# Two pre-norm layers on one core: batch 2's norm and router ahead of the expert blocks, a shared half moved between the two batches

## The chip, the cores and the metric

The kernel runs on 1 core of one Trainium2 chip. The time is the device time of one execution in microseconds; 906.62 us is the median of three runs of the kernel before (905.75 to 911.3).

## What is computed

Input: 2 sequences (batches) of 1024 tokens with 128 features. Four steps follow, each with a layer norm in front and a residual add behind:

```python
x = x + _L0_attn_ref(_layernorm(x), ...)   # latent attention, 8 heads, softmax over 1024 keys
x = x + _L0_ffn_ref(_layernorm(x), ...)    # shared expert + 2 of 8 routed experts, width 352
x = x + _L1_attn_ref(_layernorm(x), ...)   # causal attention with rotary positions, 16 heads of 8
x = x + _L1_ffn_ref(_layernorm(x), ...)    # per batch 2 of 8 experts, chosen by token 0
```

The second step is `silu(x @ gate.T) * (x @ up.T) @ down.T` for the shared expert and, by a softmax router, for the top two experts of each token, weighted by their normed probabilities. The third step needs queries, keys and values of `x` after the second.

## The kernel before

The 2048 tokens are 16 tiles of 128, and four chunks of 512 (c = 0 to 3; chunks 0 and 1 are batch 1, chunks 2 and 3 batch 2). Each engine has its own instruction list, written out by hand, and the lists meet only in semaphore waits. So the place of a call in each of the five lists sets the order of the work.

**The routed experts.** A router (`gate_logits` on PE, `probabilities`, `probabilities_normed`, `ranks`, `slots`, `block_experts`, `shares` on DVE, `gate_exps` on ACT, `expert_counts` on PE) gives each token two slots in a list that is sorted by expert and padded to blocks of 128. GpSimd (POOL) scatters the normed rows to memory (`scatter`, L580, 16 indirect DMAs a batch). 23 blocks a batch (`NB`), 46 in all (`N_ALL`), then run one after the other: SyncE loads them in quads of four blocks (`load`, L453, and `store`, L462, alternate in one queue), PE turns a quad (`block_x_turns`, L1435), ACT and DVE split it in a high and a low part (`block_x_hi`, `block_x_lo`), and for each block PE makes gate and up (`block_up`, six matmuls), ACT the silu (L939), DVE the product (`block_hidden`, L2250), PE turns it (`block_h_turns`) and multiplies down (`block_down`), ACT copies the result (`block_y`). In the loop over i (L1481, L954, L2257), block i + 1's gate and up are issued ahead of block i's turns. The weights' low parts are subtracted on POOL (`low_weights`, L572, L577) before the first block. The norm of batch 2, its turns (`second_turns`, L1223), logits and router stand inside the loop, at the blocks that `XNT_AT`, `GATE_AT`, `SOFTMAX_AT`, `RANKS_AT`, `COUNTS_AT`, `SLOTS_AT`, `EXPERTS_AT` and `SHARES_AT` name (L163).

**The shared expert** goes by chunks: `shared_up(c)` (L1377, six matmuls of 512 columns), `shared_silu` (L902), `shared_hidden` (L2115), `shared_down(c)` (L1390, 24 matmuls of 128 columns), `shared_add` (L2123). Chunks 0 and 1 come before the blocks, 2 and 3 behind them (L1490 to L1665).

**The fronts.** When a batch's blocks are stored, POOL gathers each token's two rows (`gather`, L588, 8 indirect DMAs a chunk), DVE mixes them into x (`mix`), norms (`norm_op`), PE turns (`front_turn`) and makes q, k and v (`front_qkv`), and the rotation follows (`front_rope` on DVE, `second_rope` on POOL). Fronts 0 and 1 stand in the loop of blocks 31 to 45 (`FRONT_MIX` and the like, L158), fronts 2 and 3 in attention units 0 to 2 (`SECOND_FRONT`, `FRONT_QKV_UNIT`).

**Attention of the second layer** runs in 8 units of four heads, units 0 to 3 for batch 1. POOL stages keys, queries and values of a unit (`stage_keys`, `stage_queries`, `stage_values`, L633 to L646), PE turns them (`turn_stack`, L1514), ACT copies them into stacks of float32r (L982, L988; the key stacks must be cleared before: `keys_zero`, L694 and L695). A unit needs the maxima of its scores first: 40 slots (`MX1`) of `scores_max1` on PE (L1544) and `maximum1` on DVE (L2307 masked, L2310 plain). `MX1_HALF` = 28 of unit 0's come ahead of it, the rest and those of the next unit go between its own score matmuls (`scores1`, L1564) as `first_slot(u, place)` paces them: a unit has ten steps (k) of four places each. ACT takes the exponentials (L1000), POOL masks the diagonal (L655), PE multiplies with the values (`values1`, L1581).

What follows in POOL's list is strictly in order: before, it is `scatter(0)`, `low_weights`, `scatter(1)`, `gather(0)`, clears, staging of units 0 and 1, `gather(1)` (16 DMAs), `stage_keys(2)`, masks.

## Time and profile before

| what | us |
|---|---|
| median of three runs | 906.62 |
| all runs | 905.75, 911.3, 906.62 |
| the profiled execution, its own time | 908.84 |
| its span, first to last instruction | 906.8 |
| PE busy (matmuls), share of the span | 805.3, 89% |
| DVE busy | 590.1, 65% |
| ACT busy | 515.9, 57% |
| POOL busy | 385.8, 43% |
| mean granted clock of TensorE, of full | 0.946 |

The span leaves out some 2 us of the execution's time around the first and the last instruction. A busy share is a mean over stages that have different limits, and waiting of an engine costs only where it is the one that the others wait for. TensorE's granted clock is one of two levels, 2.4 GHz (1.00) and 1.2 GHz (0.50); a value between is a mean over a stretch with both. In a timeline row, the first number is the start from the span's begin, the second the time from the first to the last of its merged instructions, and the brackets give how long the engine stood before it and who released it.

### The profile page before, as it was taken

How to read it: one execution, taken by the hardware profiler on the slowest of the kernel's cores; microseconds unless marked ns; L12 is line 12 of the kernel's file. 1: busy time of each engine (PE TensorE's matmuls, PEld its weight loads, DVE VectorE, ACT ScalarE, POOL GpSimd, SP SyncE). 2: the span in 40 equal slices, each digit the busy share in tenths (PEclk: the TensorE clock that was granted, in tenths of full speed). 3: DMA queues.
4: the chain of work that ended last, by engine and by line, in shares of the span. 5: the costliest groups of instructions: out<-in, count | busy, mean ns of one | idle time of the engine just before them, and what ended most of it. 6: DMA issues, size and time to landing. Idle time of an engine off the chain costs nothing. (4 is left out here: it accounts for less than half of the span.)

```text
span 906.8 us, 13841 instructions
## 1 busy us (share of the span) xinstructions
PE 805.3 (89%) x4634; PEld 471.4 (52%) x4634; DVE 590.1 (65%) x1552; ACT 515.9 (57%) x891; POOL 385.8 (43%) x420
## 2 busy tenths in 40 slices
PE   5889899998999988868799977899999999999858
PEld 2354343443444432568798654455555555554436
DVE  5967677686776826536326567887778778776151
ACT  3335565656656665336465533467776777676641
POOL 3406675666754754821542375236444223112100
PEclk9979999999999989989899997699999999999969
DMA  9400000000000000101232002000000000000001
GB/s 355 154 1 0 1 1 1 1 1 1 1 1 1 1 1 10 61 12 56 82 97 65 35 19 76 1 1 1 2 0 2 1 1 1 1 1 1 1 0 47
DMA packets 13789, 24.86 MB, mean 27 GB/s; under 512 B 3319, under 2 KB 8313, under 8 KB 13466
## 3 DMA queue, kind: packets, MB, share of 16 engines
q1 hardware_dynamic: 11048, 18.36, 5.8%
q0 software_dynamic: 2048, 4.20, 1.5%
q10 hardware_dynamic: 626, 1.43, 0.5%
q8 instruction: 40, 0.66, 0.3%
q14 instruction: 27, 0.22, 0.1%
HBM read 14.54 MB, written 9.44 MB: 26 GB/s over the span
## 5 line engine op out<-in xcount | busy, mean ns | idle before, releaser
L1854 DVE TENSOR_REDUCE mx_part<-ps 128x1 f32<-128x512 f32 x256 | 163.2, 681 | 68.3 <-PE ps L1166 67.5
L1000 ACT ACTIVATE pt<-ps 128x1024 f32<-128x1024 f32 (+1 forms) x160 | 149.4, 939 | 75.1 <-PE ps L1564 73.9
L795 ACT ACTIVATE pt<-ps 128x512 f32<-128x512 f32 x256 | 141.1, 596 | 85.1 <-PE ps L1191 77.1
L1544 PE MATMUL ps<-rounded 128*128 128x512 f32 (+3 forms) x384 | 140.1, 403 | 15.7 <-DVE mx_part L2307 7.6
L738 ACT ACTIVATE rounded<-ps 128x512 fp32r<-128x512 f32 (+3 forms) x166 | 97.9, 591 | 86.8 <-PE ps L1520 24.6
L2307 DVE CUSTOM_DVE_ANT_0 ps<-ps,later 128x128 f32<-128x128 f32 (+3 forms) x256 | 119.9, 516 | 26.8 <-PE ps L1544 25.4
L1191 PE MATMUL ps<-rounded 100*128 100x512 f32 x256 | 123.0, 494 | 13.5 <-ACT pt L795 12.6
L1564 PE MATMUL ps<-rounded 128*128 128x512 f32 (+3 forms) x384 | 130.1, 379 | 0.0
L655 POOL TENSOR_SCALAR_AFFINE_SELECT pt<-pt 128x512 f32<-128x512 f32 x64 | 40.0, 638 | 189.4 <-ACT pt L1000 189.4
L1166 PE MATMUL ps<-rounded 98*128 98x512 f32 x256 | 104.2, 425 | 11.2 <-DVE rounded L1847 7.7
L1544 PEld LDWEIGHTS ps<-rounded 128*128 128x128 f32 x384 | 71.8, 198 | 55.2 <-DVE mx_part L2310 22.6
L2310 DVE TENSOR_REDUCE mx_part<-ps 128x1 f32<-128x512 f32 x128 | 82.3, 685 | 23.9 <-PE ps L1544 23.8
L1564 PEld LDWEIGHTS ps<-rounded 128*128 128x128 f32 x384 | 70.8, 194 | 43.5 <-issue 19.9
L1191 PEld LDWEIGHTS ps<-rounded 100*128 100x128 f32 x256 | 48.0, 192 | 84.8 <-ACT pt L795 48.5
L533 POOL TENSOR_TENSOR xn<-pt 128x512 f32<-128x512 f32 x48 | 60.5, 1283 | 59.2 <-ACT pt L795 59.2
L1581 PE MATMUL ps<-pt,v_cur 128*9 128x512 f32 (+3 forms) x768 | 78.5, 497 | 1.5 <-POOL pt L655 1.5
L1199 PE MATMUL ps<-pt,ckv 128*32 128x512 f32 x512 | 74.3, 655 | 0.9 <-ACT pt L795 0.9
L533 POOL TENSOR_TENSOR xnT<-pt 128x512 f32<-128x512 f32 x48 | 60.5, 1281 | 33.3 <-ACT pt L795 33.3
L1166 PEld LDWEIGHTS ps<-rounded 98*128 98x128 f32 x256 | 49.1, 194 | 36.3 <-issue 17.4
L584 POOL DMA_INDIRECT to_experts<-xn,slot_i x32 | 31.8, 994 | 55.5 <-DVE slot_i L2082 46.4
L2250 DVE TENSOR_TENSOR pt<-ps,pt 128x352 f32<-128x352 f32 x46 | 24.1, 523 | 46.4 <-ACT pt L939 43.8
L738 ACT ACTIVATE pt<-ps 128x128 f32<-128x128 f32 (+2 forms) x96 | 37.5, 393 | 26.4 <-PE ps L1465 14.2
(286 smaller groups left out, 1250.3 us busy)
## 6 DMA issues: line engine op xcount, KB each, us to landing
wm<-in_wm SPq DMA_DIRECT2D x1, 4896.0 KB, 15.7
to_experts<-kstage SPq DMA_DIRECT2D x6, 512.0 KB, 4.6
of_experts<-pt SPq DMA_DIRECT2D x12, 256.0 KB, 2.0
kstage<-to_experts SPq DMA_DIRECT2D x10, 256.0 KB, 3.4
wm<-in_experts SPq DMA_DIRECT2D x1, 1028.0 KB
x<-in_x SPq DMA_DIRECT2D x4, 256.0 KB, 5.8
out<-x SPq DMA_DIRECT2D x4, 256.0 KB, 2.3
early<-in_wo ACTq DMA_DIRECT2D x1, 512.0 KB
```

The lines of the kernel that those rows point to most:

```text
L533: nc.gpsimd.tensor_tensor(sums(u, j)[i], pt0(0, i), pt0(1, i), ALU.add).then_inc(pair_add, 1)
L738: return nc.scalar.activation(dst, src, ACT.Copy)
L795: nc.scalar.activation(pt0(k, i), ps[:, ST0_BANKS[i % 2], :], ACT.Exp, scale=SCALE0).then_inc(exp_done, 1)
L1000: nc.scalar.activation(pt[:, 4 * (t % 2) + 2 * g:4 * (t % 2) + 2 * g + 2, 0:w], ps[:, ST1_BANKS[2 * g]:ST1_BANKS[2 * g] + 2, 0:w], ACT.Exp ...
L1166: mm(ps[:, max_bank(u, n), :], cq[0:NZ, b * S + j * P:b * S + (j + 1) * P], key_stack[u % 2][0:NZ, h, c * CH:(c + 1) * CH], start=True, st ...
L1191: mm(ps[:, ST0_BANKS[i % 2], :], key_stack[pp][0:NZM, h, k * P:(k + 1) * P], query_stack[pp][0:NZM, h, c * CH:(c + 1) * CH], start=True, s ...
L1544: ins = mm(bank[:, o:o + w], query_stack1[pp][:, i * P:(i + 1) * P], key_stack1[pp][:, r, c * CH:c * CH + w], start=(o == 0), stop=(o == p ...
L1564: ins = mm(ps[:, ST1_BANKS[r], o:o + w], key_stack1[pp][:, r, j * P:(j + 1) * P], query_stack1[pp][:, q0:q0 + w], start=(o == 0), stop=(o ...
L1581: ins = mm(ps[RS * r:RS * r + DH + 1, CTX_BANK, CH - w:CH], v_cur[pp][:, j, r, :], pt[:, 4 * (t % 2) + r, o:o + w], start=(j == CTX1_START ...
L1854: v.tensor_reduce(mx_part[u % 2][:, o:o + 1], ps[:, max_bank(u, n), :], AX_X, ALU.max).then_inc(max_done, 1)
L2307: v.tensor_tensor_reduce(tile, tile, later[:, CH - w:CH], 1.0, NEG, ALU.add, ALU.max, dst).then_inc(max1_done, 1)
L2310: v.tensor_reduce(dst, tile, AX_X, ALU.max).then_inc(max1_done, 1)
```

## The change

- `norm_chunk(2)`, `norm_chunk(3)`, batch 2's turns, its logits and its softmax leave the loop of the blocks and stand ahead of it; `block_x_turns(0)` goes in front of the wait for the weights' low parts. Ranks, counts, slots, experts and shares of batch 2 move from blocks 6 to 12 to blocks 0 to 6.
- Chunk 2's shared half moves from behind the blocks to between block 22 and block 23 (`SHARED_AT`); there, block 22 is finished (turned, multiplied down, copied) before block 23's gate and up. Chunk 3's up part begins at block 45, its down part lies between the first stack turns.
- Fronts 0 and 1 come two blocks sooner, so that all of front 1, rotation included, lies in the loop. Front 3's mixes and norm are done two steps a place from place 33; the turns and q/k/v of fronts 2 and 3 shift by some places.
- POOL: unit 0's keys are staged ahead of the clears; one of the two key stacks is cleared by ACT; unit 1's staging comes behind `gather(2)`; `gather(3)` is split in pairs behind unit 0's first masks, with `stage_keys(2)` after the third pair.
- `first_slot` gives unit 0 five maxima a step instead of six, over more steps, and two of them come ahead of the unit.

The core of the diff:

```diff
 def first_slot(u, place):
-    return MX1_HALF + place + (2 * HG if u else min(2 * HG, (place + 1) // 2))
+    return MX1_HALF + place + (2 * HG if u else 2 + min(2 * HG - 2, place // HG))
...
-FRONT_MIX, FRONT_STATS, FRONT_RSTD, FRONT_XN = ((31, 32), (37, 38)), (33, 39), ((34, 35), (40, 41)), (36, 42)
-FRONT_TURN, FRONT_QKV, FRONT_ROPE = (36, 42), (37, 43), (43, 46)
-
-FRONT_QKV_UNIT = {(6, 1): 0, (7, 1): 1, (8, 0): 2, (9, 1): 3}
-SECOND_FRONT = {2: (4, 2), 3: (20, 1)}
-XNT_AT, GATE_AT, SOFTMAX_AT, RANKS_AT, COUNTS_AT, SLOTS_AT, EXPERTS_AT, SHARES_AT = (1, 2), 3, (4, 5), (6, 7), 8, 9, 10, (11, 12)
+FRONT_MIX, FRONT_STATS, FRONT_RSTD, FRONT_XN = ((29, 30), (35, 36)), (31, 37), ((32, 33), (38, 39)), (34, 40)
+FRONT_TURN, FRONT_QKV, FRONT_ROPE = (34, 40), (35, 41), (41, 44)
+
+SECOND_TURN = {(0, 6, 1): 2, (1, 6, 0): 3}
+SECOND_QKV = {(0, 7, 1): (2, 0), (0, 8, 0): (2, 1), (0, 9, 1): (2, 2), (1, 1, 1): (2, 3),
+              (1, 6, 1): (3, 0), (1, 7, 1): (3, 1), (1, 8, 0): (3, 2), (1, 9, 1): (3, 3)}
+SHARED_AT = {NB - 1: 2, N_ALL - 1: 3}
+SECOND_FRONT = {2: (6, 2), 3: (33, 2)}
+RANKS_AT, COUNTS_AT, SLOTS_AT, EXPERTS_AT, SHARES_AT = (0, 1), 2, 3, 4, (5, 6)
...
@@ POOL
             gather(0)
+            gather(1)
...
             pool.wait_ge(x_turn, Q_ALL)
             nc.gpsimd.memset(kstage[1][:].bitcast(F32), 0.0).then_inc(stage_fixed, 1)
+            pool.wait_ge(rope_step, 2 * (NCH // B) - 1)
+            pool.wait_ge(stage_fixed, 1)
+            stage_keys(0, 0)
             pool.wait_ge(bu_mm, N_ALL)
-            nc.gpsimd.memset(qstage[1][:].bitcast(F32), 0.0).then_inc(stage_fixed, 1)
...
             nc.gpsimd.memset(key_stack1[0].bitcast(F32), 0.0).then_inc(keys_zero[0], 1)
-            nc.gpsimd.memset(key_stack1[1].bitcast(F32), 0.0).then_inc(keys_zero[1], 1)
...
             stage_values(0, 0)
+            nc.gpsimd.memset(qstage[1][:].bitcast(F32), 0.0).then_inc(stage_fixed, 1)
+            gather(2)
...
             stage_keys(1, 1)
             stage_queries(1, 1)
             stage_values(1, 1)
-            gather(1)
...
                 for k in range(K1_FIRST):
                     mask(u, k)
+                    if u == 0 and k < TC:
+                        if k == TC - 1:
+                            stage_keys(2, 0)
+                        gather(3, [k])
...
@@ ACT
             shared_silu(1)
+            second_xnT(2)
+            second_xnT(3)
...
             block_x_hi(0)
+            gate_exps(1)
             block_silu(0)
...
                 if n == 0:
-                    shared_silu(3, [1])
+                    act.wait_ge(bu_mm, N_ALL)
+                    act.wait_ge(consts, N_CONST)
+                    copy(key_stack1[1].rearrange("p r n -> p (r n)"), zero[:].broadcast_to([P, HG * S])).then_inc(keys_zero[1], 1)
...
+            for i in range(2):
+                act.wait_ge(y_store[i], 16 * B * NQ // 2)
             max_rows1(0, 0, 0)
...
@@ PE
             shared_down(0)
+            second_turns(2)
+            second_turns(3)
             shared_down(1)
+            gate_logits(1, 0)
+            gate_logits(1, 1)
...
+            block_x_turns(0)
             pe.wait_ge(w_lo_ok, E0)
             pe.wait_ge(block_ok, 1)
-            block_x_turns(0)
...
-                if i:
+                if i and i != NB:
                     block_down(i - 1)
...
+                if c == 2:
+                    block_down(i)
+                    block_x_turns(NQ)
+                    shared_up(2, [2])
+                    shared_down(2)
+                    pe.wait_ge(block_ok, B)
+                    block_up(NB)
...
@@ DVE
             half_var(1, 1)
+            quick_estimate(1)
             shared_hidden(1, 1)
+            quick_newton(1)
             shared_hidden(1, 2)
+            quick_newton(1)
+            quick_newton(1)
+            dve.wait_ge(half_step, hs.n)
+            norm_chunk(2)
+            norm_chunk(3)
             shared_add(0)
             shared_add(1)
+            probabilities(1)
...
             for n in range(MX1_HALF):
                 maximum1(0, 0, n)
-                if n == 1:
-                    shared_hidden(3, 2)
-                if n == 4 + 2 * TC - 1:
+                if n == 6:
                     shared_add(3)
             split_max1(0, 0, 0)
+            for n in range(MX1_HALF, first_slot(0, 0)):
+                maximum1(0, 0, n)
```

## Rows read from the trace of the kernel before

**Rows 1.** Busy by stretch: length; PE, PEld, DVE, ACT, POOL; granted clock; DMA; GB/s.

```profile
512.00:545.00 33.00, 26.22 (x126) 16.43 (x124) 18.71 (x50) 12.38 (x26) 25.39 (x31) 1.00 0.10 26
545.00:580.00 35.00, 28.64 (x100) 17.25 (x101) 26.88 (x88) 13.08 (x18) 12.82 (x17) 0.63 0.13 45
731.00:767.00 36.00, 34.56 (x232) 19.61 (x228) 28.55 (x92) 26.08 (x35) 10.03 (x19) 1.00 0.00 1
```

**Rows 2.** Timeline ahead of the blocks: start, us, engine, line, idle before.

```profile
377.62 13.10 POOL L577 TENSOR_TENSOR rounded<-wm,rounded 128x704 fp32r<-128x704 f32 x8
...
390.77 1.12 PE L1440 MATMUL ps<-ident,kstage 128*128 128x128 f32 x4 [5.60 <-POOL rounded L577]
...
397.21 0.53 DVE L2250 TENSOR_TENSOR pt<-ps,pt 128x352 f32<-128x352 f32 x1
```

**Rows 3.** Timeline of POOL's staging copies, beside DVE's rotations and after.

```profile
523.81 0.84 POOL L633 COPY xn<-big 128x256 f32<-128x256 f32 x1 [4.80 <-issue]
...
527.41 0.40 POOL L633 COPY xn<-big 128x256 f32<-128x256 f32 x1
```

**Rows 4.** Timeline of DVE, block products 10, 11, 15 and 21.

```profile
420.82 0.52 DVE L2250 TENSOR_TENSOR pt<-ps,pt 128x352 f32<-128x352 f32 x1 [1.89 <-ACT pt L939]
...
425.91 0.52 DVE L2250 TENSOR_TENSOR pt<-ps,pt 128x352 f32<-128x352 f32 x1
...
433.49 0.52 DVE L2250 TENSOR_TENSOR pt<-ps,pt 128x352 f32<-128x352 f32 x1 [0.64 <-ACT pt L939]
...
445.79 0.53 DVE L2250 TENSOR_TENSOR pt<-ps,pt 128x352 f32<-128x352 f32 x1 [1.44 <-ACT pt L939]
```

**Rows 5.** Timeline of ACT, a table load among the blocks.

```profile
408.80 1.28 ACT L830 ACT_TABLE_LOAD   x1
```

**Rows 6.** Timeline between the batches: quad 6's turns, block product 23.

```profile
450.75 1.11 PE L1440 MATMUL ps<-ident,kstage 128*128 128x128 f32 x4 [5.07 <-DMA kstage<-to_experts]
...
457.33 0.53 DVE L2250 TENSOR_TENSOR pt<-ps,pt 128x352 f32<-128x352 f32 x1 [1.41 <-ACT pt L939]
```

**Rows 7.** Timeline of POOL, one scatter of batch 2.

```profile
428.64 0.96 POOL L584 DMA_INDIRECT to_experts<-xn,slot_i  x1 [0.30 <-issue]
```

**Rows 8.** Timeline of PE, matmuls of a shared half.

```profile
512.36 1.88 PE L1387 MATMUL ps<-xnT,wm 128*128 128x512 f32 x4
...
521.72 2.94 PE L1401 MATMUL ps<-wm,pt 128*128 128x128 f32 x24 [0.85 <-DVE pt L2121]
```

**Rows 9.** Timeline from the last block product to unit 0's first score matmul.

```profile
511.02 0.52 DVE L2250 TENSOR_TENSOR pt<-ps,pt 128x352 f32<-128x352 f32 x1
...
515.49 3.51 POOL L695 MEMSET rounded<- 128x4096 f32 x1
...
527.34 0.54 PE L1520 MATMUL ps<-identr,kstage 128*128 128x128 f32 x4 [2.67 <-POOL kstage L641]
...
545.65 9.64 DVE L2310 TENSOR_REDUCE mx_part<-ps 128x1 f32<-128x512 f32 x16
...
557.99 0.76 PE L1564 MATMUL ps<-rounded 128*128 128x512 f32 x1
```

**Rows 10.** Line L1000 of ACT: durations min/median/max by shape.

```profile
L1000 ACT ACTIVATE pt<-ps x160: 592/1024/1055, 560.1 to 852.6; 128x1024 f32<-128x1024 f32 x128, 128x512 f32<-128x512 f32 x32
```

**Rows 11.** Busy time and granted clock, block 0 and unit 0.

```profile
392.00:396.00 4.00, 2.60 (x9) 2.61 (x10) 2.86 (x14) 0.99 (x2) 0.00 (x0) 0.50 0.17 66
560.00:580.00 20.00, 17.95 (x68) 11.29 (x69) 15.20 (x64) 8.38 (x12) 2.50 (x4) 0.50 0.00 1
```

**Rows 12.** Timeline of unit 0: mask 2, the stack turn, fifth step's first scores.

```profile
577.17 0.64 POOL L655 TENSOR_SCALAR_AFFINE_SELECT pt<-pt 128x512 f32<-128x512 f32 x1 [5.78 <-ACT pt L1000]
...
585.18 0.54 PE L1520 MATMUL ps<-identr,kstage 128*128 128x128 f32 x4
585.55 0.47 PE L1564 MATMUL ps<-rounded 128*128 128x512 f32 x1
```

234 lines of the change are left out of this document (114 added, 120 removed).

## The prediction

> **What bounds the kernel now.** I read the page first for the busy shares, then a table of stretches, then the timelines of the stretches that the diff touches. The page shows TensorE (PE) busy 89% of the span (the table above), so each stretch has to be asked what stops PE there. The stretches [rows 1] answer: a late attention unit (731 to 767) has PE busy 34.56 of 36 us at full clock, and nothing in the diff changes its work. Three stretches are worse. From 512 to 545, the end of the expert blocks, PE is busy 26.2 of 33 us while POOL is busy 25.4. From 545 to 580 the granted clock is 0.63, which is a mix of its two levels (2.4 and 1.2 GHz), and VectorE (DVE) is busy 26.9 of 35. Before them the blocks have a hole of their own (term C). I therefore add up six terms, each a distance between two instructions of before, and compare each with what the new order should give. "Hidden n" is block n's product on DVE (L2250); it marks the pace of the blocks, 46 of them.
>
> **A, ahead of the blocks.** POOL ends its eight weight products at 377.62 + 13.10 = 390.72, and only then PE turns the first rows, 5.60 us idle [rows 2]. Hidden 1 comes at 397.21, 6.5 us after POOL. The change puts the turns of quad 0 in front of that wait, and batch 2's norm, turns and gate logits in front of the turns. PE's added work there is small against the idle time: eight transposes and sixteen small matmuls, some 3 us. Then only the two blocks' twelve matmuls (1.9 us), a silu (0.47) and a step or two of latency lie behind POOL, 3.5 us, so hidden 1 would be at 394.2: -3.0. Against it, DVE's eight norm scalings and two additions now run beside POOL's products. No row of before shows those two together; the nearest is a POOL copy that took 0.84 us beside DVE's rotations and 0.40 without [rows 3]. I charge 1.0 us for that, for a sum of **-2.0**, bounds 0 (POOL's products slow by the whole gain) and -3.5. The Trainium skill (GPSIMD Engine Reference, section 8, Key points) says that GpSimd shares its SBUF interfaces with VectorE, with contention when a DVE instruction has two SBUF inputs; the additions read PSUM and SBUF and the scalings one tensor, so by the rule the charge would be near 0. For the rotations, which do read two, the trace agrees with the rule (0.84 for 0.40).
>
> **B, blocks 1 to 21.** Hidden 15 at 433.49 and hidden 21 at 445.79 [rows 4] give the clean pace: 12.30 / 6 = 2.05 us. From hidden 1 to hidden 21 before took 445.79 - 397.21 = 48.6, against 20 x 2.05 = 41. The 7.6 us over are: batch 2's turns and logits on PE; two table loads on ScalarE (ACT) of 1.28 us each with an exponential of 0.3 between, 2.9 us [rows 5]; and the slot computation, where hidden 10 to 11 took 425.91 - 420.82 = 5.09, 3.0 over the pace [rows 4]. The first two leave the loop: the loads then fall beside the last POOL products and block 0's matmuls. The slot chain (DVE L2052 to L2083, 3.4 us) stays, but no longer shares its block with a quad's low part (0.69), and the blocks behind it catch up: I count 1.5 for it and 0.8 for ranks and counts, so 43.3 and **-5.3**. Bounds -3 (ranks, counts and slots now follow each other in blocks 0 to 3, with nothing stored up ahead of PE) and -7. The Trainium skill (ScalarE: Activation LUTs, What ACT_TABLE_LOAD costs) gives about 2.66 us for each switch, with its drain; two would be 5.3. The trace shows 1.28 for a load and no drain behind it, so the row is taken; by the page the term would be some 2.4 us larger.
>
> **C, between the batches.** Before, PE stands 5.07 us for quad 6's load, whose rows POOL had only just scattered, and resumes at the lower clock (the turns take 1.11 for 0.6); hidden 21 to 23 took 457.33 - 445.79 = 11.5 for a normal 4.1 [rows 4, 6]. In the new kernel the slots are ready some 19 us sooner (block 3 instead of 9), so POOL's 16 scatters at 0.96 + 0.30 = 1.26 us each [rows 7] end near 427 and the load lands about 10 us before it is needed. The wait is gone; what is late next is the shared half itself. It is six matmuls of 512 columns and 24 of 128. Four of the first took 1.88 and 24 of the second 2.94, ends included [rows 8], so 2.6 + 2.6 = 5.2 us of PE, and the pipeline drains: PE waits for silu (0.6), DVE (0.7) and hops between the last up and the down, 1.8 us, and again 0.4 before block 23's turns. With block 22's turns and down brought forward, hidden 22 to 23 becomes 11.0, so the two steps are 13.05: **+1.5**. Bounds -0.5 (the silu finds cover) and +4 (one more drain, by the same rows). The PE work is not extra: it leaves the end.
>
> **D, blocks 23 to 45.** The order is the same except that fronts come two blocks sooner, so two more q/k/v matmuls with their copies fall in front of hidden 45 instead of behind. Each such block costs 0.6 over the pace: 384 columns for PE, which are three quarters of a 512-column matmul pair [rows 8], and their two copies. **+1.2**, bounds 0 and +2.5. The gathers feeding the first front start near 448 instead of 463 and land before they are wanted, so no wait there. Sum so far -4.6: hidden 45 at 506.4 for 511.02.
>
> **E, from hidden 45 to the first score matmul (L1564) of attention unit 0.** Before: 557.99 - 511.02 = 47.0 [rows 9]. PE's first stack turn stood for POOL's staging (2.67 us) at 527.34, 16.3 after hidden 45, since rotations and POOL's clears (up to 519.0) came first, and a whole shared half (5.2 us) lay in the way. New: the third rotation starts 2.0 after hidden 45 and takes 2.1, staging 3.5: first stack turn at +7.7. POOL clears one stack (3.51), to +11.1; ACT stacks four keys (2.4) to 13.6; queries staged by 13.5 and stacked by 14.9. First maxima at +15.5 (before: +22.5). ACT now clears the second stack. Its copy of 4096 columns has no row; an exponential of 512 columns took 0.592 us and one of 1024 1.024 [rows 10], 0.84 per 1000 columns, so 3.6; bounds 2.5 and 5. Its keys are then stacked at +21.2 and PE's fourth stack turn waits for that, maxima 6 to 27 follow: 3.7 + 0.7 (add) + 9.64 [rows 9] + 0.8 (split), then the turn, its copy and one more turn, 2.1: +39.6 at full clock. But PE stands from about +9.7 to +13.7. It fell to the lower clock after 5.6 us idle ahead of the blocks and after 5.07 us between the batches, and not after 2.67 us [rows 1, 2, 6, 9, 11]; I charge 2 us for half clock in this stretch: 41.6, **-5.4**, bounds -1 and -9. POOL's gather(2), now ahead of unit 1's staging, is 8 x 1.26 = 10.1 us from about +15; staging 1 is then done at +30, and PE wants its keys at about +33: covered by 3 to 5 us, and if the cover fails each late us costs one.
>
> **F, unit 0.** Its first four steps took 585.55 - 557.99 = 27.6 us, at half clock for the most part [rows 9, 12], against 3.6 for a step of a late unit (36 us for ten). DVE had six maxima per step there and the mixes of front 2 beside them; the new pacing gives five per step and starts the mixes later: I count 20 maxima for 24 at 1.15, -5 (with the two done ahead). Of this, the two steps after them get a maximum more each (+1.2) and front 3's mixes, two per place from place 33, cost about 2 us in the last two steps. On POOL, a gather pair (2.5 us) follows each of the first masks, and stage_keys(2) comes behind mask 2 and its pair: staged 5.1 us after the mask. PE asked for it 585.18 - 577.81 = 7.4 us after that mask at the slow pace [rows 12], so it is hidden there, and would cost up to 3 at full pace. I take **-2.0**, bounds +5 and -7.
>
> Units 1 to 7 and the tail: 0. **Sum:** -2.0 - 5.3 + 1.5 + 1.2 - 5.4 - 2.0 = -12.0. The profiled execution took 908.84 (span 906.8 and 2.0 around it), which gives 896.8; it lies 2.2 above the median of the runs, 906.62, so the prediction for the median is **894.6**.
>
> **The rivals.** (1) *The clock takes E and F back.* Two new idle stretches for PE behind the blocks (waits for clears and for the second stack), and DVE-bound maxima that leave PE under its share, so half clock lasts through unit 0 as it did before: E -2, F 0, sum -6.6, 900.0. For: from 560 to 580 PE was busy 18 of 20 us and stayed at half clock [rows 11]. Against: fewer maxima per step, so PE is denser. Chance 0.14. (2) *The clock comes back early.* F runs at 4.2 us per step: F -6, A without my charge, E at +39.6: sum -19, 887.6. Chance 0.16. (3) *The router's early chain starves the blocks.* Ranks, counts and slots in the first four blocks, or a scatter that ends too late, so that the load at the boundary still waits: B -2 and C +4, sum -6.2: 900.4. It is also the case that the change doesn't do what it says. For: DVE has nothing ahead of it in blocks 0 to 3. Against: 10 us of room. Chance 0.06. (4) *POOL's queue becomes the bound; slower than before.* The gathers are 16 x 1.26 = 20.2 us, in POOL's one queue in front of unit 1's staging, between unit 0's masks and in front of unit 2's keys. If all are on the path, -12.0 + 20.2 = +8.2: 914.8. It decides from 12 us exposed. For: PE waited for POOL's staging already (2.67). Against: POOL is busy 12.8 of 35 us from 545 to 580 [rows 1]. Chance 0.05. The forecast keeps 0.59.
>
> **How the numbers follow.** The forecast's own spread, from terms that don't all err one way, is 889 to 900. The range reaches to rivals 1 and 3 above and to 2 below: 886 to 903. About 1% (9 us) is what a measurement of this kernel can tell from no change, so faster means below 897.6. All of rival 2 lies there, 0.86 of the forecast (its centre is 3 us below the line) and a third of rivals 1 and 3: 0.16 + 0.51 + 0.07 = 0.74. Rival 4 and a little of what is outside all cases make slower 0.06; the rest is same, 0.20.
>
> **What would show it.** A: the first turn of quad 0 before POOL's last product, hidden 1 less than 4.5 us behind it. B: no ACT table load among the blocks; hidden 21 near 438.5. C: no DMA wait at a quad's turn, 24 shared down matmuls between hidden 22 and 23, 13 us from 21 to 23. E: first stack turn within 9 us of hidden 45; L1564's first 42 us behind it. F: the first four steps of unit 0 under 24 us. Wrong if PE's waits in unit 0 name POOL staging or masks with more than 5 us, or if the granted clock from the last block to the end of unit 0 stays at its lower level longer than before.

## The result, and where the time went

The changed kernel took 905.6 us in the median of 20 runs (904.42 to 907.55), the kernel before 910.4 on the same chip (905.75 to 914.71): ratio 0.9936, 95% interval 0.9919 to 0.9953. The gain is clear of the noise and small: 0.6% by the ratio, 4.8 us between the medians. 894.6 was forecast, 12.0 us under the three runs known then (a ratio of 0.987), so the measured time lies 11.0 us above the forecast. In the profiled executions it is 905.09 (span 903.2) against 908.84 (906.8), 3.75 us less. The page shows the same picture as before, share by share (PE 89% then and now, granted clock 0.945 for 0.946):

```profile
PE 801.9 (89%) x4634; PEld 469.6 (52%) x4634; DVE 601.6 (67%) x1552; ACT 518.8 (57%) x892; POOL 380.7 (42%) x419
```

So the shares tell nothing of where the time went. The rest of this section is read from these two traces in the six distances of the forecast. "Turned maxima" is PE's turn of a unit's maxima (`turn_max1`), after which that unit's scores can start.

| distance | before | forecast | changed |
|---|---|---|---|
| A: hidden 1 (second of a pair of products at 404.72) | 397.21 | 395.2 | 405.2 |
| B: hidden 1 to 21 | 48.6 | 43.3 | 45.2 |
| C: hidden 21 to 23 | 11.5 | 13.05 | 15.0 |
| D: hidden 23 to 45 | 53.7 | 54.9 | 53.6 |
| E: hidden 45 to the first score matmul | 47.0 | 41.6 | 40.55 |
| F: from there to the first turned maxima of unit 1 | 49.4 | 47.4 | 42.8 |

A is 10 us off, more than twice as much as any other. It stands in this timeline of the changed kernel (start, us, engine, line, operation, idle before), where [rows 2] had PE alone waiting for POOL:

```profile
377.70 13.07 POOL L583 TENSOR_TENSOR rounded<-wm,rounded 128x704 fp32r<-128x704 f32 x8
...
377.83 1.57 DVE L1795 TENSOR_SCALAR lnv<-lnv 128x8 f32<-128x8 f32 x1
379.32 0.16 DVE L1796 TENSOR_SCALAR lnv<-lnv 128x8 int32<-128x8 int32 x1
379.51 1.53 DVE L1798 TENSOR_SCALAR lnv<-lnv 128x8 int32<-128x8 int32 x1
380.95 0.68 DVE L2147 TENSOR_TENSOR pt<-ps,pt 128x512 f32<-128x512 f32 x1
...
382.71 1.59 DVE L1805 TENSOR_TENSOR lnv<-lnv 128x8 f32<-128x8 f32 x1
384.33 1.59 DVE L1807 SCALAR_TENSOR_TENSOR lnv<-lnv 128x8 f32<-128x8 f32 x1
...
391.23 0.17 DVE L1807 SCALAR_TENSOR_TENSOR lnv<-lnv 128x8 f32<-128x8 f32 x1
...
391.44 2.14 DVE L1772 TENSOR_SCALAR xn<-x,mv,lnv 128x128 f32<-128x128 f32 x8
...
392.61 2.14 PE L1248 MATMUL ps<-ident,xn 128*128 128x128 f32 x8 [10.03 <-DVE xn L1772]
394.54 3.94 PE L1416 MATMUL ps<-wm,pt 128*128 128x128 f32 x24
398.31 1.85 PE L1254 MATMUL ps<-gw,xnT 128*128 128x8 f32 x16
```

POOL's eight products of 1.63 us run from 377.70 to 390.77. Beside them DVE computes batch 2's reciprocal root in small operations. L1807 takes 1.59 us there for eight columns; behind POOL's end the same form takes 0.17. The chain of 12 operations, with two shared products in it, lasts 13.6 us (377.83 to 391.40), and PE stands 10.03 us for the norm. So quad 0's turns come not ahead of POOL's last product, as forecast, but at 400.02, and hidden 1 is 14.4 us behind POOL where [rows 2] had 6.5. ACT's two table loads with the exponential between them (401.31 to 404.15) now also lie ahead of block 0's silu, which starts at 404.17 though PE is done with its matmuls at 403.4. Eight of the twelve operations take 1.1 to 1.6 us. Not every one is stretched: the product that reads PSUM (L2147) takes its 0.68, and the shift L1796 gets through in 0.16 right behind one that was held. Theory: **a DVE operation whose tensors all lie in SBUF is held until the POOL instruction beside it ends**, one per POOL instruction. Rivals: the two engines share the memory at a fixed rate; the waits between the small operations cost the time; or PE's added work (the turns and the logits, with the second shared down between them, 392.6 to 400, granted clock 0.50 up to 396) sets hidden 1 by itself.

C comes next. Between the batches there is no DMA wait, as forecast, but the shared half is larger than I had it:

```profile
453.07 1.88 PE L1402 MATMUL ps<-xnT,wm 128*128 128x512 f32 x4
...
455.12 1.88 PE L1402 MATMUL ps<-xnT,wm 128*128 128x512 f32 x4
...
458.61 1.88 PE L1402 MATMUL ps<-xnT,wm 128*96 128x512 f32 x4
461.34 2.94 PE L1416 MATMUL ps<-wm,pt 128*128 128x128 f32 x24 [0.85 <-DVE pt L2147]
```

Twelve records of 512 columns, four for each third, and not six.

In E the parts came where the forecast had them: first stack turn 7.8 us behind hidden 45 (forecast 7.7), ACT's clear of 4096 columns 3.61 us (3.6), POOL's staging of unit 1 done 4.9 us before PE turned its keys:

```profile
532.71 3.61 ACT L749 ACTIVATE rounded<-zero 128x4096 fp32r<-128x4096 f32 x1
...
547.67 0.42 POOL L654 COPY v_cur<-early 128x288 f32<-128x288 f32 x1
...
552.94 0.46 PE L1540 MATMUL ps<-identr,kstage 128*128 128x128 f32 x4
```

The granted clock did not come as forecast. Its lower level, charged with 2 us, held for most of the stretch (the busy table: length; PE, PEld, DVE, ACT, POOL; granted clock; DMA; GB/s), where the kernel before had 1.00 in the same window:

```profile
535.00:550.00 15.00, 12.07 (x37) 8.30 (x36) 10.16 (x32) 4.15 (x6) 10.98 (x18) 0.50 0.32 102
```

PE's longest wait before it fell was 2.40 us (at 531.67), less than the 2.67 us that the prediction took as harmless. What this cost in E is not measured by itself; run 7's trace has E at 38.9 us with a mean granted clock of 0.86 over it, for 40.55 with 0.76 here.

F gained three times what I gave it. The busy table has for 560 to 580 a clock of 0.90 where [rows 11] has 0.50; ahead of the blocks the lower level is the same:

```profile
392.00:396.00 4.00, 3.39 (x15) 3.08 (x16) 2.18 (x8) 1.20 (x2) 0.00 (x0) 0.50 0.00 0
...
560.00:580.00 20.00, 17.73 (x101) 11.45 (x100) 17.73 (x80) 12.73 (x17) 12.56 (x17) 0.90 0.09 24
```

Unit 1 gives 1.3 us back (between its first turned maxima and unit 2's: 39.8 us for 38.4); from there on the lead stays at 3.7.

### The profile page after: what moved, and what is told of

Read it like the earlier page. It is cut to its first block, busy times and chain, and to the rows that moved or that the text cites. A ratio compares the mean times of both kernels' runs of the same rounds, so it can differ in the third digit from the quotient of the medians.

```text
span 903.2 us, 13842 instructions
## 1 busy us (share of the span) xinstructions
PE 801.9 (89%) x4634; PEld 469.6 (52%) x4634; DVE 601.6 (67%) x1552; ACT 518.8 (57%) x892; POOL 380.7 (42%) x419
## 4 chain that ended last, share of the span: by engine, by line
PE 62%; DVE 23%; ACT 7%; issue 4%; POOL 3%; DMA 1%; ACTq 0%; SPq 0%; POOLq 0%; DVEq 0%
PE ps L1564 7%; PE ps L1601 6%; PE ps L1206 6%; PE ps L1214 6%; PE ps L1181 5%; DVE ps L2339 5%; PE ps L1584 4%; DVE mx_part L2342 4%; PE ps L1492 3%; PE ps L1222 3%; DVE mx_part L1882 3%; ACT rounded L749 3%; PE ps L1170 2%; DVE cT L1905 2%; PE ps L1474 2%
## 5 line engine op out<-in xcount | busy, mean ns | idle before, releaser
L1564 PE MATMUL ps<-rounded 128*128 128x512 f32 (+3 forms) x384 | 138.8, 399 | 16.1 <-DVE mx_part L2339 8.3
L749 ACT ACTIVATE rounded<-ps 128x512 fp32r<-128x512 f32 (+3 forms) x166 | 97.7, 590 | 67.8 <-PE ps L1170 19.7
L1584 PE MATMUL ps<-rounded 128*128 128x512 f32 (+3 forms) x384 | 127.9, 373 | 0.0
L1564 PEld LDWEIGHTS ps<-rounded 128*128 128x128 f32 x384 | 71.4, 197 | 55.5 <-DVE mx_part L2342 22.8
L1584 PEld LDWEIGHTS ps<-rounded 128*128 128x128 f32 x384 | 69.2, 190 | 41.7 <-issue 18.9
## 6 DMA issues: line engine op xcount, KB each, us to landing
wm<-in_wm SPq DMA_DIRECT2D x1, 4896.0 KB, 15.7
```

What stands on the lines that cost most here:

```text
L749: return nc.scalar.activation(dst, src, ACT.Copy)
L1564: ins = mm(bank[:, o:o + w], query_stack1[pp][:, i * P:(i + 1) * P], key_stack1[pp][:, r, c * CH:c * CH + w], start=(o == 0), stop=(o == p ...
L1584: ins = mm(ps[:, ST1_BANKS[r], o:o + w], key_stack1[pp][:, r, j * P:(j + 1) * P], query_stack1[pp][:, q0:q0 + w], start=(o == 0), stop=(o ...
```

## The experiments

Fifteen runs were made in four sets. The kernel before ran in each set on the same chip: 947.77 us in the first, 913.95 in the second, 948.97 in the third, 910.62 in the fourth. On the chips of the first and third, all kernels, the one before too, had stops of some 10 us in the blocks that the trace gives to no instruction of the program, as this one of ACT in the first run:

```profile
439.99 0.49 ACT L751 ACTIVATE pt<-ps 128x384 f32<-128x384 f32 x1 [8.03 <-remote]
```

These stops hide other waits: in run 4, the kernel before with a probe, hidden 21 to 23 takes 4.6 us there, without the wait for quad 6's load, for 11.5 in the first trace. So a ratio of these two sets can't be held against one of the other two, and the changed kernel itself ran in the second alone. I compare ratios inside a set, and, ahead of the blocks, times from the last value of batch 2's variance (DVE's 128x8 operation at 377.53 before, 377.64 in the changed kernel) to hidden 1: **19.7 us before, 27.5 in the changed kernel.**

**1. POOL's products in quarters.**

```diff
-nc.gpsimd.tensor_tensor(w_lo[:, e, :], wm[:, e, 0:2 * F0], w_hi[:, e, :]..., ALU.subtract).then_inc(w_lo_ok, 1)
+for o in range(0, 2 * F0, 176):
+    ins = nc.gpsimd.tensor_tensor(w_lo[:, e, o:o + 176], wm[:, e, o:o + 176], w_hi[:, e, o:o + 176]..., ALU.subtract)
+ins.then_inc(w_lo_ok, 1)
```

> POOL's eight weight products are cut into quarters of 176 columns; nothing else changes against the changed kernel. Theory (held): each small DVE operation of batch 2's rstd chain ends only when the POOL instruction beside it ends, so with POOL instructions of about 0.4 us the nine held operations of 1.1 to 1.6 us become 0.4 us or less each; the chain ends near 384, the norm scalings near 387, PE's turns run before POOL ends (about 391), hidden 1 comes at 395 to 398 instead of 405.2, and the time falls by 6 to 9 us against the changed kernel (896.5 to 899.5). Rival 1 (shared bandwidth): DVE gets a fixed share of SBUF beside POOL, whatever the length of POOL's instructions; the operations stay at 1.1 to 1.6 us, hidden 1 stays within 1 us of 405.2, the time within 1 us. Rival 2 (PE's added work): turns, shared down and gate logits set hidden 1; DVE's operations get short but hidden 1 stays above 403.

Measured: 943.36 us, ratio 0.995 (0.9931 to 0.9969). The changed kernel did not run in this set, so the distances have to tell. In the timeline:

```profile
379.03 16.46 POOL L584 TENSOR_TENSOR rounded<-wm,rounded 128x176 fp32r<-128x176 f32 x32
...
386.83 0.48 DVE L1807 TENSOR_TENSOR lnv<-lnv 128x8 f32<-128x8 f32 x1
...
391.45 4.13 DVE L1774 TENSOR_SCALAR xn<-x,mv,lnv 128x128 f32<-128x128 f32 x8
```

The same small operation takes 0.48 us beside POOL instructions of 0.51 (16.46 / 32), where it took 1.59 beside 1.63. That rules out a shared rate. The scalings, which in the changed kernel lay behind POOL, are held too: one every 0.52 us for one every 0.27. But POOL's cut products take 3.4 us longer, and the norm still ends together with POOL (395.5), so hidden 1 comes 25.5 us after the variance, 2 us sooner than in the changed kernel. The 7 to 10 us that I expected there did not come: I had not counted the scalings as held, and on this chip the variance came 4.7 us after POOL's start (0.1 us before it in the changed kernel's trace), so that more of the norm fell late beside POOL.

**2. POOL waits for the chain.**

```diff
 pool.wait_ge(pv_mm, U0 * TS)
+pool.wait_ge(half_step, N_HALF + 12)
```

> POOL's first product waits for the last step of batch 2's rstd chain; nothing else changes against the changed kernel. Theory (held): the chain's operations take 0.17 us each and end near 381; POOL then runs from 381 to 394.2. The eight norm scalings (128x128 float32, SBUF only) now fall beside POOL's products; if they are held as the small operations were, each takes about 1.6 us, the last ends near 394, and hidden 1 stays at 404 to 408: no gain, time within 3 us of the changed kernel's. If scalings are not held, they end near 384 and hidden 1 follows POOL by 3.5 to 4: 398, -7 us. Rival (PE's added work): hidden 1 follows POOL's end by 13 us as it does now whatever DVE does: 407 to 408.

Measured: 947.97 us, ratio 0.9988 (0.9961 to 1.0015): not to be told from the kernel before, and 4.6 us above run 1 beside it.

```profile
388.63 0.17 DVE L1804 TENSOR_TENSOR lnv<-lnv 128x8 f32<-128x8 f32 x1
...
389.23 11.71 DVE L1773 TENSOR_SCALAR xn<-x,mv,lnv 128x128 f32<-128x128 f32 x8
...
389.44 13.06 POOL L584 TENSOR_TENSOR rounded<-wm,rounded 128x704 fp32r<-128x704 f32 x8 [10.04 <-DVE lnv L1808]
```

The chain is back at 0.17 us an operation, with all its waits, one every 0.20 us: they are not the cost. Now the eight scalings pay, 11.71 us for 2.14. Hidden 1 comes 29.0 us after the variance and 10.6 behind POOL's end.

**3. Batch 2's norm back in the blocks**; all other parts of the change kept.

```diff
-RANKS_AT, COUNTS_AT, SLOTS_AT, EXPERTS_AT, SHARES_AT = (0, 1), 2, 3, 4, (5, 6)
+XNT_AT, GATE_AT, SOFTMAX_AT, RANKS_AT, COUNTS_AT, SLOTS_AT, EXPERTS_AT, SHARES_AT = (1, 2), 3, (4, 5), (6, 7), 8, 9, 10, (11, 12)
...
-block_x_turns(0)
 pe.wait_ge(w_lo_ok, E0)
 pe.wait_ge(block_ok, 1)
+block_x_turns(0)
...
+if i in XNT_AT:
+    second_turns(QH + XNT_AT.index(i))
+if i == GATE_AT:
+    gate_logits(1, 0); gate_logits(1, 1)
```

> Batch 2's norm, turns, gate logits and softmax go back into blocks 0 to 5, and ranks, counts and slots into 6 to 9, as in the kernel before; quad 0's turns again behind the wait for POOL. The rest of the change stays. Theory (held): the hold costs about 10 us and the loop part brought 3.4, so undoing both gives hidden 1 at 397.2 (405.2), hidden 21 near 446 (450.4), hidden 23 near 461 since quad 6's rows are wanted only behind block 22's down, and the time 4 to 5 us below the changed kernel, 900 to 902. Rival (the router's early chain carries the gain at the boundary): the load for quad 6 is late again, 5 us, and the time is that of the changed kernel or above it.

Measured: 937.07 us, ratio 0.9884 (0.9849 to 0.9918), the lowest of this set. The load for quad 6 is not late (hidden 21 to 23: 15.5 us), so the rival falls as far as a trace with stops can tell; run 14 has 15.2 without them. The size of the gain is taken up again in run 14.

**4. A probe in the kernel before.**

```diff
 shared_add(0)
+hs.mark(v.tensor_scalar(row[1], row[0], -0.5, None, ALU.mult))
+hs.mark(v.tensor_copy(row[2], row[0]))
+...
 shared_add(1)
```

> The kernel before with seven small DVE operations of 128x8 added in the idle time beside POOL's weight products (382.5 to 390.7), nothing taken away: a float32 scaling, a float32 copy, an int32 shift, a scaling that reads PSUM, then a product of two SBUF tiles, a reduction, and another product. Theory (held): the float32 operations with SBUF operands alone take up to a POOL instruction (1.6 us), the shift and the one that reads PSUM about 0.17; hidden 1 moves by less than 1 us since the block's first low part is wanted only at 392.5. Rival (the waits in the chain, not POOL): operations that wait for nothing take 0.17 each.

Measured: 946.32, one run, beside 947.77. Its placing missed: PE was late on this chip, and only the first operation fell beside POOL (1.44 us); the others ran behind it at 0.15 to 0.16. Run 9 repeats it further ahead.

**5. The changed kernel once more.**

> The changed kernel once more, as it is, so that the kernels of this set have it beside them on their own chip. Ratio to the kernel before 0.990 to 0.997 as measured first (0.9936).

Measured: 905.38 us, ratio 0.9918 (0.9892 to 0.9943).

**6. Chain first, scalings on ACT.**

```diff
+pool.wait_ge(half_step, 2 * N_HALF)
...
+act.wait_ge(half_step, 2 * N_HALF)
+for t in range(TS, NT):
+    second_xn(t)
...
-quick_estimate(1); shared_hidden(1, 1); quick_newton(1); shared_hidden(1, 2); quick_newton(1); quick_newton(1)
-norm_chunk(2); norm_chunk(3)
+quick_rstd(1); shared_hidden(1, 1); shared_hidden(1, 2)
```

`second_xn` is ACT's Identity with scale and bias by row, as the kernel has it for batch 1; `quick_rstd` makes the bias as its last operation.

> Against the changed kernel: DVE runs batch 2's rstd chain in one piece with one operation more (minus mean times rstd), POOL's first weight product waits for it, and the eight norm scalings go to ACT (scale and bias per row, 0.4 us each). No DVE operation with SBUF operands alone is left beside POOL's products. Theory (held): chain about 3 us, so POOL's products start and end 3 us later than in the changed kernel (377.7 and 390.8 there); ACT's scalings, PE's turns, shared down and logits all fall beside them, and hidden 1 follows POOL's end by 3.5 to 4.5 us instead of 14.4: 7 to 8.5 us earlier than in the changed kernel, and the time 6 to 9 us below it (ratio to the kernel before 0.984 to 0.987). Rival (PE's added work): hidden 1 still follows POOL's end by 13 to 14 us, so it comes 3 us later than in the changed kernel and the time is 2 to 4 us above it.

Measured: 898.54 us, ratio 0.9839 (0.9808 to 0.987), 6.8 us below the changed kernel beside it, within what was expected. Hidden 1 comes 21.0 us after the variance and 5.0 behind POOL's end, somewhat more than the 3.5 to 4.5 expected; run 13 shows why.

**7. Scalings stay on DVE, POOL waits for them.**

```diff
+pool.wait_ge(ln_xn, 2 * NT)
```

> Against the changed kernel: POOL's first weight product waits for the last of DVE's eight norm scalings; the scalings stay on DVE. Theory (held): with nothing beside it the chain takes 3 us and the scalings 2.1, with two shared products between; POOL starts 6 to 8 us later than in the changed kernel, and hidden 1 follows its end by 3.5 to 4.5 us: 2 to 4 us earlier than in the changed kernel; time 2 to 4 us below it. Rival (PE's added work): hidden 1 and the time 6 to 8 us later than in the changed kernel.

Measured: 901.22 us, ratio 0.9876 (0.984 to 0.9912), 4.2 below the changed kernel; hidden 1 24.6 us after the variance and 5.0 behind POOL's end. Counted from the variance, POOL starts 6.5 us later than in the changed kernel, and nothing else in the program is different; yet hidden 1 is 2.9 us earlier. PE does all its turns, shared downs and logits beside POOL in this kernel. The rival of PE's work is out: it delays hidden 1 only when the held norm pushes it behind POOL. Not all of the 4.2 us comes from there: E took 38.9 us in this trace, at a mean granted clock of 0.86, and 40.7 at 0.72 in the changed kernel beside it.

**8. The old pacing of maxima.**

```diff
-return MX1_HALF + place + (2 * HG if u else 2 + min(2 * HG - 2, place // HG))
+return MX1_HALF + place + (2 * HG if u else min(2 * HG, (place + 1) // 2))
```

> Against the changed kernel only first_slot goes back to its form before (unit 0 takes one more of the next unit's maxima at every second place from place 0, six maxima a step, instead of one at every fourth with two done ahead). If the pacing gave unit 0's gain (first four steps 19.0 us instead of 27.6, the unit 46.0 instead of 52.2): the first four steps go back to 23 to 28 us and the time rises by 4 to 6 us. If it was the granted clock, which is higher ahead of unit 0 in the changed kernel, or the later start of front 2's mixes: the first four steps stay below 22 us and the time within 2 us.

Measured: 912.68 us, ratio 1.0008 (0.9982 to 1.0033), 7.3 above the changed kernel beside it: the pacing alone is worth more than the whole net gain of the change. The first four steps take 27.0 us (18.9 in the changed kernel beside it), within the 23 to 28 expected; the time rose by more than the 4 to 6 expected. From the first score matmul to the turn in the fourth step it takes 23.6 us (before 24.2, changed kernel 15.7), to unit 1's first turned maxima 49.0 (49.4, 42.8). The busy table from 560 to 565, first of run 5, then of run 8:

```profile
560.00:565.00 5.00, 4.86 (x20) 3.80 (x19) 3.93 (x16) 4.51 (x6) 0.98 (x2) 0.62 0.00 0
```

```profile
560.00:565.00 5.00, 4.35 (x15) 3.05 (x15) 3.23 (x14) 3.47 (x4) 0.00 (x0) 0.50 0.00 0
565.00:570.00 5.00, 4.83 (x16) 3.86 (x15) 3.37 (x14) 2.64 (x4) 2.59 (x3) 0.50 0.10 26
```

Both enter the unit at the lower level. With five maxima a step in the way in place of six, PE has no stop there up to 565; with the old pacing the timeline has waits of 0.17 to 0.33 us for DVE's `mx`. The clock is back at full level by 565 with the new pacing, and still at 0.50 up to 570 with the old. The expectation put pacing and clock as alternatives; they go together here, since these two kernels differ by the pacing alone. How the 8 us of the first four steps divide into work removed and clock is not measured.

**9. The probe, better placed**, in the kernel before, right behind the variance.

```diff
 half_var(1, 1)
+hs.mark(v.tensor_scalar(row[1], row[0], -0.5, None, ALU.mult))
+hs.mark(v.tensor_scalar(row[2], row[0], -0.5, None, ALU.mult))
+hs.mark(v.tensor_scalar(row[3].bitcast(I32), row[0].bitcast(I32), 1, None, ALU.logical_shift_right))
+hs.mark(v.tensor_copy(row[4], row[0]))
 shared_hidden(1, 1)
...
```

> The kernel before with eight operations of 128x8 added on DVE right behind batch 2's variance, where POOL's products have just begun: two float32 scalings, an int32 shift, a float32 copy, then (behind a shared product that reads PSUM) a reduction, a reciprocal and two float32 products of two SBUF operands. The changed kernel's trace has the scaling, the product and the three-operand form at 1.1 to 1.6 us beside POOL and the shift at 0.16; a copy, a reduction and a reciprocal it does not have. Theory: whatever is held ends with a POOL instruction, 1.63 us apart; what is not held takes 0.15 to 0.2. The scalings and the products are held, the shift and the shared product (0.68) not; the copy, like the scaling, reads one float32 tile and should be held, the reduction and the reciprocal not. Hidden 1 moves by less than 1.5 us. Rival (the waits between the operations, not POOL): operations that follow one another with no wait between them take 0.17 each.

Measured (one run, 953.26 beside 948.97):

```profile
386.27 1.60 DVE L2146 TENSOR_SCALAR lnv<-lnv 128x8 f32<-128x8 f32 x1
387.78 1.72 DVE L2147 TENSOR_SCALAR lnv<-lnv 128x8 f32<-128x8 f32 x1
389.41 1.71 DVE L2148 TENSOR_SCALAR lnv<-lnv 128x8 int32<-128x8 int32 x1
391.04 1.72 DVE L2149 COPY lnv<-lnv 128x8 f32<-128x8 f32 x1
392.67 0.68 DVE L2121 TENSOR_TENSOR pt<-ps,pt 128x512 f32<-128x512 f32 x1
393.27 0.14 DVE L2153 TENSOR_REDUCE lnv<-lnv 128x1 f32<-128x8 f32 x1
393.34 0.18 DVE L2154 RECIPROCAL lnv<-lnv 128x8 f32<-128x8 f32 x1
393.45 0.93 DVE L2155 TENSOR_TENSOR lnv<-lnv 128x8 f32<-128x8 f32 x1
394.30 0.15 DVE L2156 TENSOR_TENSOR lnv<-lnv 128x8 f32<-128x8 f32 x1
```

```profile
381.28 13.08 POOL L577 TENSOR_TENSOR rounded<-wm,rounded 128x704 fp32r<-128x704 f32 x8
```

POOL's instructions end at 381.28 + 1.635 n: 387.82, 389.46, 391.09, 392.73, 394.36. The first four operations, between which nothing waits, end at 387.87, 389.50, 391.12 and 392.76, each within 0.05 us behind one of these, and the product L2155 at 394.38. The rival of the waits is out. I was wrong about the shift: it is held as the others are (in the changed kernel it had slipped through behind a held one; why is open). The copy and the scalings, which read one tensor, are held like the product, which reads two. The reduction, the reciprocal and the product that reads PSUM are not; the first two rest on one operation each. A second expectation was missed as well: hidden 1 was to move by less than 1.5 us, and comes 17.6 us after the variance, for 14.6 in run 10 on the same chip.

**10. Norm in the blocks, again.**

> The kernel of the third run again (batch 2's norm, turns, logits and softmax in blocks 0 to 5 as before the change, ranks, counts and slots behind them, the rest of the change kept), since in its first set long stops without a releaser lay in the blocks. Theory: hidden 1 back near 397.2, hidden 1 to 21 back to 48.6, 21 to 23 stays at 15.0 without a wait for the load, so hidden 23 is 4 to 5 us earlier than in the changed kernel and the time 900 to 902 (ratio to the kernel before 0.986 to 0.989). Rival (without the early router the load for quad 6 is late again): 21 to 23 takes 18 us or more and the time is within 2 us of the changed kernel's.

Measured: ratio 0.9861 (0.9834 to 0.9888), hidden 21 to 23 15.6 us. The stops lay in the blocks again (hidden 1 to 21 took 67 us).

**11. As run 6, and DVE takes three of the eight products.**

```diff
+NLOW = 5
...
-for e in range(E0):
+for e in range(NLOW):
     low_weights(e)
...
+low_product(NLOW)
 shared_add(0)
+low_product(NLOW + 1)
+low_product(NLOW + 2)
 shared_add(1)
```

`low_weights` is POOL's, `low_product` the same subtraction on DVE.

> The kernel of the sixth run (chain first, scalings on ACT), with the last three of the eight weight products given to DVE, which stands idle there. If a held DVE operation ends with a POOL instruction and does not slow POOL, POOL's five products end 8.2 us after the chain instead of 13.1 and DVE's three end in their shadow or soon behind (1.6 us each while held). Then PE's turns, logits, ACT's two table loads and the low part bound: hidden 1 comes 3.5 to 4.5 us earlier relative to the end of the chain than in the sixth run, 894 to 896. If DVE's large products and POOL's slow each other, so that the eight take 13 us together: no gain, 898 to 900.

Measured: ratio 0.988 (0.9853 to 0.9907). POOL's five took 10.17 us where run 12's five, with no DVE product beside them, took 8.19: POOL is held as well. Run 15 has it on another chip.

**12. As run 10, with three products on DVE.**

> The kernel of the tenth run (norm in the blocks), with the last three weight products on DVE. POOL's five end at about 385.8 instead of 390.8, DVE's three (two of them beside POOL, 1.6 us each) by 387; PE's shared down ends near 385.5, so hidden 1 comes near 391.5, 5 to 6 us earlier than in the tenth run, and PE does not stand long enough to lose its clock: 894 to 897. If the engines slow each other: 900 to 902 as the tenth run.

Measured: ratio 0.9861 (0.9831 to 0.9891), as run 10, and not the 894 to 897 us expected. PE was late on this chip (a wait of 4.4 us for DVE), so DVE's products lay behind POOL's and nothing was decided. This version was not tried on another chip.

In this set the order of the norm made no difference that can be told: 936.43 us in run 10 (norm in the blocks), 937.92 in run 11 (norm ahead). The variance came some 5 us after the moment at which run 10's POOL began, and run 11's POOL waits for it: hidden 1 comes 17.8 us after the variance for 14.6, which takes back most of the 3.9 us that the blocks gain.

**13, 14, 15: runs 6, 10 and 11 side by side** on a chip where the kernel before took 910.62.

> The sixth run's kernel again (norm ahead, chain before POOL's products, scalings on ACT), beside the next two on one chip. Ratio to the kernel before 0.982 to 0.987; hidden 1 comes 21 us after batch 2's variance, hidden 1 to 21 takes 45 us.

> The tenth run's kernel again (norm in the blocks). If the forecast's idea was right and only the hold spoilt it: hidden 1 comes 19.7 us after the variance, as before the change, 1 us earlier than in the kernel beside it, but hidden 1 to 21 takes 48.5 for 45, so that the time is 2 to 3 us above it (ratio 0.985 to 0.990). If the early norm is worth nothing even when it is not held: the time within 1 us of it or below.

> The eleventh run's kernel again (as the first of this set, three of the eight products on DVE). There the two engines took 10.2 us for the eight in place of 13.1. If POOL's products set the start of the blocks: hidden 1 comes 17.8 us after the variance for 21, and the time is 2.5 to 3.5 us below the first of this set. If something else does (the table loads, the low part, the clock): less than 1 us below it.

| | time | ratio (95%) | variance to hidden 1 | hidden 1 to 21 | 21 to 23 | 23 to 45 |
|---|---|---|---|---|---|---|
| 13 norm ahead, off DVE | 898.88 | 0.9862 (0.9828 to 0.9896) | 21.0 | 44.7 | 15.0 | 53.5 |
| 14 norm in the blocks | 903.22 | 0.9908 (0.9873 to 0.9944) | 19.7 | 48.7 | 15.2 | 55.2 |
| 15 as 13, DVE takes three products | 896.15 | 0.9835 (0.9799 to 0.9871) | 18.1 | 44.7 | 15.0 | 53.5 |

On this chip the early norm is worth 4.3 us over the norm in the blocks once it is not held, more than the 2 to 3 expected (six executions each, 897.43 to 900.34 and 900.92 to 905.89). The traces give 1.3 lost ahead, 3.9 gained in blocks 1 to 21 and 1.7 in 23 to 45. The last part lies in blocks 42 to 44, where run 14's granted clock fell (0.51 from 508 to 511) and run 13's did not (1.00 in the same blocks); that this comes from the order is not shown. What is left for the order in these traces is 2.6. The changed kernel, with the hold, gained no more than run 14 (ratio 0.9918 in the second set, 0.9908 here). Run 13 ahead of the blocks:

```profile
379.83 3.19 ACT L833 ACTIVATE xn<-x,lnv 128x128 f32<-128x128 f32 x8 [0.68 <-DVE lnv L1819]
...
380.03 13.09 POOL L584 TENSOR_TENSOR rounded<-wm,rounded 128x704 fp32r<-128x704 f32 x8 [2.92 <-DVE lnv L1819]
...
394.14 0.66 PE L1478 MATMUL ps<-rounded 128*128 x1 [5.55 <-issue]
394.59 0.49 PE L1479 MATMUL ps<-rounded 128*128 x1
...
398.13 0.53 DVE L2282 TENSOR_TENSOR pt<-ps,pt 128x352 f32<-128x352 f32 x1 [1.20 <-PE ps L1480]
```

ACT's scalings follow one another every 0.40 us beside POOL's products of 1.63; ACT is not held. Chain 2.9, POOL 13.1, 5.0 behind it make the 21.0. Those 5.0 are more than the 3.5 of the forecast since PE stood 5.55 us and ran blocks 0 and 1 at half clock (0.49 a matmul, 0.32 at full). Run 15, the fastest in its set, ahead of the blocks:

```profile
381.90 10.17 POOL L585 TENSOR_TENSOR rounded<-wm,rounded 128x704 fp32r<-128x704 f32 x5 [2.98 <-DVE lnv L1820]
...
382.78 1.55 DVE L2164 TENSOR_TENSOR rounded<-wm,rounded 128x704 fp32r<-128x704 f32 x1
...
384.86 4.05 DVE L2164 TENSOR_TENSOR rounded<-wm,rounded 128x704 fp32r<-128x704 f32 x2
```

Eight products in 10.2 us for 13.1, hidden 1 2.9 us earlier and the time 2.7 us lower, as expected (894.6 to 900.01 in six executions, so the two ranges still touch): they set the start of the blocks. POOL's five take 1.68, 2.34, 2.33, 2.32 and 1.67 us, and the three long ones are those in which a DVE product ends; DVE's alone take 0.88 in run 12. So POOL waits for DVE's instructions as well, 2.0 us in all; two engines on the same memory gained 2.9 us, not the 4.9 of a free split. The clock fell here too (0.52 from 391 to 397), in a wait of PE of only 2.63 us.

## Why the prediction was wrong, point by point

**A (forecast -2.0, measured +8.0) is the step that failed.** The forecast's sentence was that DVE's "eight norm scalings and two additions now run beside POOL's products", with 1.0 us charged for it. Two things were missing. The twelve operations of the rstd chain, which also move there, were not in that list, although everything behind them waits for them in turn. And [rows 3] were read for what DVE's rotations cost POOL; the cost that mattered is POOL's to DVE. The trace of before has it in the same stretch: two of the rotation's products ahead of POOL's copies, then the same two beside them:

```profile
522.19 0.41 DVE L2235 TENSOR_TENSOR half<-big,sin 128x256 f32<-128x256 f32 x1
522.52 0.42 DVE L2236 TENSOR_TENSOR half<-big,sin 128x256 f32<-128x256 f32 x1
...
524.31 0.62 DVE L2235 TENSOR_TENSOR half<-big,sin 128x256 f32<-128x256 f32 x1
524.85 0.83 DVE L2236 TENSOR_TENSOR half<-big,sin 128x256 f32<-128x256 f32 x1
```

It is not a slower rate but a wait for the end of a whole instruction, so it falls hardest on the shortest: 13.6 us for a chain that takes 4.0 in run 7, 9.6 us lost. Runs 1, 2, 7 and 9 show the hold, runs 6 and 13 what is left without it.

Of the Trainium skill's rule (GPSIMD Engine Reference, section 8, Key points) I had used one half, contention when a DVE instruction has two SBUF inputs, and it gave "near 0" for the scalings; run 2 has them at 11.71 us for 2.14, with one SBUF tensor read. The other half of the same sentence, a DVE instruction in a two-port performance mode, I had left out, and another page says how the contention works: by the Trainium skill (SBUF — State Buffer, section "SBUF: two separate sides") the shared ports are an exclusive lock, kept for a whole instruction, not a split of bandwidth; and by the Trainium skill's page "VectorE: DVE Perf Modes" (Mode 2×_2P, and the perf-mode tier table) a float32 scaling or copy in SBUF can run in such a mode, and a reduction has the plain one alone. The traces agree but for one shift that slipped through: operations end with POOL's instructions (run 9), quartering those shortens them (run 1), scaling and copy are held and the reduction is not (run 9), and POOL is delayed in its turn (run 15).

In numbers of the forecast: at up to one POOL product of 1.63 us for a held operation, the chain's twelve operations outlast the eight products of [rows 2], so the norm could only end behind POOL. PE's added work was rightly counted at nothing as long as it is covered (run 7). Uncovered, the stretch from the norm's end to hidden 1 was 11.6 us: 6.4 for the turns, a shared down and the logits, partly at the lower clock, and 5.1 from quad 0's turns to hidden 1, in which block 0's silu also waited for ACT's table loads.

**B (-5.3, measured -3.4).** The two table loads left the loop, as forecast; run 14 beside 13 gives the move -3.9. Blocks 2 to 10 now take 19.4 us for 16.4 at the clean pace, where ranks, counts and slots now are; from hidden 1 to 21 it is 4.2 over the pace, for which I had 2.3.

**C (+1.5, measured +3.4): a mis-sized term.** The wait for the load went, as the forecast said. But "six matmuls of 512 columns" at four for 1.88 us: [rows 8] have four records for one third of the up part, which is two matmuls in the code; the three thirds are twelve records and 5.3 us, not 2.6. The drains cost about 0.8 us less than I had. A count of records must be held against a count of calls.

**D (+1.2, measured -0.1):** just outside its bounds of 0 and +2.5; the two more q/k/v matmuls cost nothing that shows (53.6 us for 53.7).

**E (-5.4, measured -6.4):** near by its parts, with two flaws. The terms written out for it add up to +38.1 and not +39.6; the 1.5 is not named there, and the trace has 1.8 us from the fourth stack turn (538.68) to the next maxima (540.48). And the 2 us for the clock rested on a reading that does not hold: the lower level came with waits of 2.40 us here and 2.63 in run 15, and lasted some 17 us, not a few; that the sum still came out near is partly luck. ACT's clear, which no row of before had, was 3.61 us for an estimated 3.6. POOL's queue was covered, by 4.9 us for a forecast 3 to 5; rival 4 did not occur.

**F (-2.0, measured -6.6).** I counted maxima and gave the clock to a rival: the clock came back some 17 us earlier than before (at 564, not at 581), and run 8 shows the pacing as its cause: without it unit 0 takes 6.3 us longer and the lower level lasts to 574. So rival 2 (the clock comes back early, -6 for F) was right for F, while its A was as wrong as mine. Unit 1 took back 1.3. Of the other rivals, 3 did not occur (no wait for the load), and 1 was wrong in its outcome: the clock was low for long in E, and both E and F gained.

By the measured terms: 8.0 - 3.4 + 3.4 - 0.1 - 6.4 - 6.6 = -5.1 at the end of unit 0, +1.3 in unit 1, against a span that is 3.6 us shorter. Against the forecast that is +10.0 in A, +1.9 each in B and C, -1.3 in D, -1.0 in E and -4.6 in F: the total is only some 8 us off because F, for a reason that the forecast did not count, took back almost half of what A lost. With A as run 13 has it (1.3 us behind the kernel before, not 8.0) the sum would be -10.5; run 13's profiled execution has a span of 895.8, 11.0 below the kernel before's 906.8.

## What to carry to other kernels

Before moving a chain of small VectorE operations beside long GpSimd instructions, list every instruction that moves, and for each whether all its operands lie in SBUF: such a one cost up to one GpSimd instruction here, whatever its size (unless it was a reduction or a reciprocal). Put the chain ahead of them, put the elementwise part on ScalarE, or let the operation read PSUM. And where two engines pace each other at TensorE's lower clock, try a pacing that takes PE's small stops out: here it was worth 7.3 us, and the clock came back 10 us sooner than with the old one. A kernel's gain in one stage on one chip need not be its gain on another: look at which engine is late there.

## What was not expected of the hardware

- A DVE scaling, copy, shift or product of 128x8 in SBUF took up to 1.5 to 1.7 us beside POOL instructions of 1.63 us and 0.48 beside those of 0.51, ending within 0.05 us of theirs; a reduction (0.14), a reciprocal (0.18), a product with a PSUM operand (0.68) and ACT's scalings (one every 0.40) were not stretched.
- It works both ways: three large DVE products made POOL's five take 10.17 us for 8.17.
- Cutting a POOL product of 704 columns into four raised it from 1.63 to 2.06 us (16.46 / 8).
- In unit 0 the full clock came back at 564 in the changed kernel and at 574 in the kernel that differs from it by the old pacing alone, where PE had small stops of 0.17 to 0.33 us.
- The clock also fell after PE had stood for only 2.40 us (behind the blocks) and 2.63 us (run 15, ahead of them); 2.67 us in the kernel before did not cost it.
